# A neural network's forward pass on one core: query and value products of the head loop from split operands

## The chip, the core and the metric

One Trainium2 chip, one core (core 0). The metric is the device time of one execution in microseconds (us). Three runs of the kernel before gave a median of 2646.47 us, from 2644.33 to 2648.1.

## What is computed

Four blocks work on an input of 4 x 128 x 32 x 32: a convolution block, a dynamic convolution, an attention with a gated feed-forward block, and the block that matters here: an attention with 16 heads on 4 x 1024 tokens of 128 channels, and a mixture of experts behind it. The reference of that attention, cut to what the change touches:

```python
cq = _rms(x @ Wcq, q_norm_w)                    # query latents, 48 a token
qn = (cq @ Wq_nope).reshape(B, T, N_HEAD, NOPE) # 32 a head, Wq_rope gives 32 more, then turned
qr = _rope((cq @ Wq_rope)...)
q = jnp.concatenate([qn, qr], -1)
ckv = _rms(x @ Wckv, kv_norm_w)                 # key/value latents, 32 a token
v1 = (ckv @ Wv).reshape(B, T, N_HEAD, VDIM)     # 32 a head
o1 = _attn(q, k1, v1, causal)                   # all earlier keys
o2 = _attn(q, ks, vs)                           # 256 selected keys
o3 = _attn(q, kw, vw, winmask)                  # a window of 64 keys
o = g[:, 0] * o1 + g[:, 1] * o2 + g[:, 2] * o3
return o @ Wproj
```

## The kernel before

The program runs in stages with a barrier behind each: `stage_conv`, `stage_attn2`, `stage_ffn2`, `stage_latents` (L1652), `stage_heads` (L2185), `stage_ffn3`. Two of them are touched.

**`stage_latents`** makes, for each of the 4 batches, the layer norm, the query and key/value latents, the gates and the selection of 256 keys, and stores all in one DRAM tensor `latents`. DVE scales the latents into `CK` (L1866 to L1874), TensorE transposes `CK` to 112 rows (L1761), ScalarE copies them to `CF` [112, 1024] (L1820); rows 0 to 31 are the key/value latents, rows 32 to 63 the mean part of the values, rows 64 to 111 the query latents, all fp32. `CKS` holds the key/value latents split in two: a high part rounded to TensorE's fast fp32 type (called fp32r in the rows) and a low part, the remainder. SP stores five tiles a batch (L1699 XC, L1702 CF, L1705 gates, L1708 CKS, L1711 XS) and waits for all of them at the end; POOL does nothing after three memsets.

**`stage_heads`** makes 16 passes: 4 batches, and in each 4 groups of four heads. The first pass and what overlaps it run ahead of a hardware loop (`nc.Fori`), whose 15 turns each end one pass and begin the next; all engines follow one order of steps written out by hand, the string `ORDER` (L1971). A step with a plus sign belongs to the next pass: the query groups stand in it as `+a.q0` (ahead of `+near` work, behind `score.17.2`), `+a.q1` (behind `score.18.3`), `+a.q2` (behind `score.24.0`) and `+a.q3` (behind `score.3.0`), the value products of the causal branch as `v.v1.0` (at `score.4.1`) and `v.v1.1` (at `score.5.3`). A query group (`group`, L2388) is two fp32 products of 256 columns, CF's 112 rows by `WQ` [112, 256], whose rows 0 to 63 are zero; the same helper makes the window's and the selected keys' groups (`WKW`, `WKS`). A value product (`value_product`, L2416) is four fp32 products of 128 columns, CF by `WV` [112, 128], with zeros outside its 32 rows. An fp32 product shows as two MATMUL records, one of fp32r operands as one.

Scores are made from split operands (L2480 and L2481: `QH`, `QL` and the keys `K`, `K1B`), ScalarE takes their exponentials (`PT`, L2621), TensorE multiplies them with the values (L2500), and POOL adds the exponentials of the causal branch over the key tiles (`KT`, L2339), which TensorE turns into denominators (L2510, with `ones`). DVE rounds, normalises and gathers (`YB`, L2722), POOL adds the branches (`YA`, `YT`, L2345, L2348). SP loads the next pass's tiles behind step `load.next` (L2275: XS, WKS, XC, WKW, WQ, WVW, WVS) and behind `load.own` (L2284: CF, CKS, gates, WK1, WV), both long ahead of their use except in the first pass. At the stage's start TensorE runs 62 products of masks (`keep_clock`, L2524) while the first loads land, and DVE clears `WQ` and `WV` (L2753, L2755).

## Time and profile before

| | |
|---|---|
| median of 3 runs | 2646.47 us (2644.33 to 2648.1) |
| the profiled execution, its own time | 2643.02 us |
| its span; mean granted TensorE clock | 2641.1 us; 0.943 of full speed |
| PE, PEld busy | 2367.4 us (90%), 1718.4 us (65%) |
| DVE, ACT, POOL busy | 1814.2 (69%), 1413.0 (53%), 1285.8 us (49%) |
| DMA | 128.14 MB; HBM read 61.26, written 20.79 MB |
| latents' stage; head stage | from 505 to 638 us; from 638 to 2470 us |

The profile is one execution. PE is TensorE's matmuls, PEld its weight loads, DVE VectorE, ACT ScalarE, POOL GpSimd, SP SyncE, which here issues the transfers. Busy shares are means over stages with different limits, so a change is judged by the stage in which it lies and by the waits there: a row of the timeline ends with the idle time before it and what ended that.

### The profile page before, as it was taken

What the parts mean: (1) busy time and instruction counts of PE and PEld (TensorE: products, weight loads), DVE (VectorE), ACT (ScalarE), POOL (GpSimd) and SP (SyncE); (2) the same over time, 40 slices, a digit from 0 to 9 for tenths busy, and PEclk for the clock granted to TensorE, in tenths of its full rate; (3) what the DMA queues carried; (4) which work ended last, traced back from release to release, by engine and by line L of the source; (5) the groups of instructions that cost most, each with busy time, mean ns of one, the idle gap of its engine ahead of it and who ended that gap; (6) DMA issues with size and microseconds to landing.
All of it is one profiled execution on the core that took longest, in us unless ns stands there. A gap on an engine that the chain in (4) does not pass through costs nothing. (4 is left out here: it accounts for less than half of the span.)

```text
span 2641.1 us, 51557 instructions
## 1 busy us (share of the span) xinstructions
PE 2367.4 (90%) x16821; PEld 1718.4 (65%) x16821; DVE 1814.2 (69%) x3640; ACT 1413.0 (53%) x2489; POOL 1285.8 (49%) x972
## 2 busy tenths in 40 slices
PE   6889968666899999999999999999999999999767
PEld 4666645454667767677676676767667676675656
DVE  5868745585577686776867768676776867766436
ACT  2135544232565656656566565665657666575223
POOL 1016760000264746647365573755737557375445
PEclk8989988768999999999999999999999999999678
DMA  3040300013412111220212202122021220210233
GB/s 118 1 102 20 78 10 1 16 50 87 129 43 54 28 41 36 49 54 16 54 36 45 58 16 54 36 45 58 16 54 36 45 58 16 54 20 17 70 118 102
DMA packets 82189, 128.14 MB, mean 49 GB/s; under 512 B 15824, under 2 KB 58240, under 8 KB 81728
## 3 DMA queue, kind: packets, MB, share of 16 engines
q1 hardware_dynamic: 77616, 119.47, 17.9%
q0 software_dynamic: 3024, 7.43, 0.9%
q8 instruction: 46, 0.75, 0.1%
q10 hardware_dynamic: 1472, 0.24, 0.1%
q14 instruction: 31, 0.25, 0.0%
HBM read 61.26 MB, written 20.79 MB: 31 GB/s over the span
## 5 line engine op out<-in xcount | busy, mean ns | idle before, releaser
L2621 ACT ACTIVATE a_PT<-PS 128x512 f32<-128x512 f32 (+1 forms) x1104 | 584.4, 565 | 365.1 <-PE PS L2486 241.4
L2339 POOL TENSOR_TENSOR a_KT<-a_PT 128x256 f32<-128x256 f32 (+2 forms) x176 | 354.3, 2025 | 459.7 <-ACT a_PT L2621 451.2
L2339 POOL TENSOR_TENSOR a_KT<-a_KT,a_PT 128x2048 f32<-128x2048 f32 (+3 forms) x128 | 391.8, 3061 | 10.3 <-ACT a_PT L2621 1.0
L2690 DVE TENSOR_REDUCE a_NM<-PS 128x2 fp32r<-128x512 f32 (+2 forms) x512 | 290.8, 612 | 134.2 <-PE PS L2430 73.5
L2480 PE MATMUL PS<-a_QH,a_K 128*128 128x512 f32 (+3 forms) x768 | 293.1, 392 | 2.9 <-ACT a_PT L2621 2.8
L2702 DVE TENSOR_REDUCE a_MX<-PS 128x1 f32<-128x512 f32 (+3 forms) x432 | 265.6, 664 | 32.7 <-PE PS L2445 18.1
L2480 PE MATMUL PS<-a_QH,a_KSW 128*128 128x192 f32 (+3 forms) x832 | 264.5, 339 | 12.1 <-DVE a_NM L2690 10.5
L2445 PE MATMUL PS<-a_K,a_QH 128*128 128x512 f32 (+3 forms) x768 | 252.3, 404 | 9.4 <-DVE a_K L2677 8.1
L2481 PE MATMUL PS<-a_QL,a_K1B 76*128 76x512 f32 (+3 forms) x768 | 260.1, 349 | 0.0
L2430 PE MATMUL PS<-a_KSW,a_QH 128*128 128x256 f32 (+2 forms) x1024 | 198.8, 306 | 4.1 <-DVE a_QL L2674 4.1
L2430 PEld LDWEIGHTS PS<-a_KSW,a_QH 128*128 128x128 f32 x1024 | 164.0, 193 | 49.6 <-DVE a_NM L2690 19.5
L2327 POOL TENSOR_TENSOR a_TM<-a_R 128x128 f32<-128x128 f32 x288 | 124.1, 458 | 130.0 <-DVE a_R L2656 130.0
L2480 PEld LDWEIGHTS PS<-a_QH,a_KSW 128*128 128x128 f32 x832 | 160.4, 193 | 41.3 <-issue 13.5
L2677 DVE TENSOR_TENSOR a_KSW<-PS,a_KSW 64x512 fp32r<-64x512 f32 x160 | 110.3, 689 | 108.3 <-ACT a_KSW L2580 105.3
L2580 ACT ACTIVATE a_QH<-PS 64x512 fp32r<-64x512 f32 x256 | 151.5, 592 | 51.3 <-PE PS L2398 46.6
L2486 PE MATMUL PS<-masks,identb 128*128 128x128 bf16 (+3 forms) x592 | 172.2, 291 | 0.0
L2480 PEld LDWEIGHTS PS<-a_QH,a_K 128*128 128x128 f32 x768 | 149.0, 194 | 33.6 <-issue 14.5
L2445 PEld LDWEIGHTS PS<-a_K,a_QH 128*128 128x128 f32 x768 | 135.6, 193 | 45.5 <-DVE a_MX L2702 17.3
L2607 ACT ACTIVATE a_QL<-PS 12x1024 fp32r<-12x1024 f32 x128 | 130.1, 1017 | 60.7 <-PE PS L2460 58.3
L2481 PEld LDWEIGHTS PS<-a_QL,a_K1B 76*128 76x128 f32 x768 | 147.1, 192 | 9.6
L2656 DVE TENSOR_TENSOR a_R<-PS,a_angles 128x512 f32<-128x512 f32 x144 | 96.2, 687 | 72.9 <-ACT a_TM L2572 71.9
L2481 PE MATMUL PS<-a_QL,a_KWB 76*128 76x192 f32 (+2 forms) x576 | 141.1, 275 | 0.0
(434 smaller groups left out, 5223.2 us busy)
## 6 DMA issues: line engine op xcount, KB each, us to landing
a_KWB<-a_KSW SPq DMA_DIRECT2D x64, 256.0 KB, 3.3
a_K1B<-a_K SPq DMA_DIRECT2D x32, 512.0 KB, 4.9
a_XC<-latents SPq DMA_DIRECT2D x16, 512.0 KB, 3.8
a_CKS<-latents SPq DMA_DIRECT2D x16, 512.0 KB, 4.6
a_CF<-latents SPq DMA_DIRECT2D x16, 448.0 KB, 4.2
slots<-in_empty_slots SPq DMA_DIRECT2D x1, 5160.0 KB, 18.7
f_XB<-slots SPq DMA_DIRECT2D x8, 645.0 KB, 6.0
c_EX<-in_experts SPq DMA_DIRECT2D x1, 4608.0 KB, 18.0
```

What stands on the lines that cost most here:

```text
L2327: last = nc.gpsimd.tensor_tensor(TM[:, x, :, 32 + c:48 + c], r[:, :, 0, c:c + 16], r[:, :, 1, other:other + 16], ALU.add)
L2339: nc.gpsimd.tensor_tensor(total, one_in, other_in, ALU.add).then_inc(s["added"], 1)
L2430: last = nc.tensor.matmul(bank[:, m * w:(m + 1) * w], QH[:, h, i * 128:(i + 1) * 128], keys[x][:, h, c0:c0 + w], start=m == 0, stop=x == 1 ...
L2445: last = nc.tensor.matmul(bank[:, m * w:(m + 1) * w], QH[:, h0 + m, i * 128:(i + 1) * 128], K1[:, h0 + m, c0:c0 + w], start=m == 0, stop=n ...
L2480: nc.tensor.matmul(out, keys[x][:, h, c:c + 128], QH[:, h, start:start + w], start=m == 0, stop=False)
L2481: last = nc.tensor.matmul(out, upper[x][0:DH + ROWS, h, c:c + 128], QL[0:DH + ROWS, h, start:start + w], start=False, stop=mask is None an ...
L2486: last = nc.tensor.matmul(by_heads[:, :, 0:cols], identb[:, :], add[:, None, :].broadcast_to([128, each, cols]), start=False, stop=True)
L2580: last = nc.scalar.activation(odd_even({"q": QH, "w": KW, "s": KS}[g[0]], e, rows, tokens(g)), ring(key)[e * DH:(e + 1) * DH, :].rearrange ...
L2607: nc.scalar.activation(QL[DH:DH + ROWS, :, p * PAIR:(p + 1) * PAIR], turning(key)[DH:DH + ROWS, None, 0:PAIR].broadcast_to([ROWS, QUAD, PA ...
L2621: nc.scalar.activation(PT[:, to:to + width], turning(key)[:, 0:width], ACT.Exp).then_inc(s["taken"], 1)
L2690: nc.vector.tensor_reduce(NM[:, i, DH:].rearrange("p (h x) -> p h x", x=3)[:, h:h + 2, x], ring(key)[:, 0:2 * w].rearrange("p (h n) -> p h ...
L2702: nc.vector.tensor_reduce(out, ring(key)[:, 0:heads * w].rearrange("p (h n) -> p h n", h=heads), AX.X, ALU.max, negate=True).then_inc(s["r ...
```

## The change

**Operands.** `stage_latents` now makes `CQ` [128, 1024], the query latents twice: the mean multiply on DVE writes them twice into `CQ2` (768 elements in place of 384), TensorE transposes 128 rows, ScalarE copies all of them rounded into `CQ` and the lower 64 rows unrounded into `CF`, and POOL subtracts, so that rows 0 to 47 hold the high part and rows 64 to 111 the low part. The weights `wq3` and `wv` are loaded whole, twice (partitions 0 and 64), rounded by four activations of ScalarE ahead of the batch loop, their low parts made by two subtractions of POOL, and both parts kept in a new DRAM tensor `parted` [128, 3072], 1.5 MB, stored by two transfers at the end of the stage.

**Products.** A query product is two fp32r matmuls that add up in one bank, CQ by the high and CQ by the low part of the weights; a value product is CKS by the two parts of `WV`. `WQ` is now [128, 2, 256] (256 KB a load, before 48), `WV` [128, 2, 128] (128 KB, before 16), CQ 512 KB (CF was 448). The two memsets of DVE go. Nothing moves in `ORDER`.

```diff
-        CF, XS, row = sb("CF", [CKW + QR_, N]), sb("XS", [C, KEEP3]), rk["row"]
+        CF, CQ, XS, row = sb("CF", [128, N]), sb("CQ", [128, N], F32R), sb("XS", [C, KEEP3]), rk["row"]
...
+        CK2, CQ2 = sb("CK2", [128, NT, 2, CKW]), sb("CQ2", [128, NT, 2, CKW])
+        WQF, WVF = sb("WQF", [128, NQ, QUAD * DH]), sb("WVF", [128, NQ, QUAD * VD])
+        WQP, WVP = sb("WQP", [128, 2, NQ, QUAD * DH], F32R), sb("WVP", [128, 2, NQ, QUAD * VD], F32R)
...
+                wq, wv = d["wq3"][0:NQ * QR_, :], d["wv"][0:NQ * KR_, :]
+                for at in (0, CKW):
+                    sp.dma_start(WQF[at:at + QR_, :, :], wq.rearrange("(g p) c -> p g c", p=QR_)).then_inc(s["ld_parted"], 16)
+                    sp.dma_start(WVF[at:at + KR_, :, :], wv.rearrange("(g p) c -> p g c", p=KR_)).then_inc(s["ld_parted"], 16)
...
-                    sp.wait_ge(s["lt_copied"], b * 2 + 2)
+                    sp.wait_ge(s["lt_split"], b + 1)
...
-                    sp.dma_start(entry[0:CKW + QR_, N:2 * N], CF[:, :]).then_inc(s["archived"], 16)
+                    sp.dma_start(entry[:, N:2 * N], CQ[:, :].bitcast(F32)).then_inc(s["archived"], 16)
...
+                sp.wait_ge(s["parted_low"], 2)
+                sp.dma_start(parted[:, 0:2 * NQ * QUAD * DH], WQP[:, :, :, :].rearrange("p a g c -> p (a g c)").bitcast(F32))\
+                    .then_inc(s["parted_kept"], 16)
+                sp.dma_start(parted[:, 2 * NQ * QUAD * DH:], WVP[:, :, :, :].rearrange("p a g c -> p (a g c)").bitcast(F32))\
+                    .then_inc(s["parted_kept"], 16)
                 sp.wait_ge(s["archived"], (B + 1) * ARCHIVE)
+                sp.wait_ge(s["parted_kept"], 32)
...
+                for tile in (WQP[:, :, :, :], WVP[:, :, :, :], CQ2[:, :, :, :]):
+                    nc.gpsimd.memset(tile.bitcast(F32), 0.0).then_inc(s["blank"], 1)
+                pool.wait_ge(s["parted_high"], 4)
+                nc.gpsimd.tensor_tensor(WQP[0:QR_, 1, :, :], WQF[0:QR_, :, :], WQP[0:QR_, 0, :, :].bitcast(F32), ALU.subtract)\
+                    .then_inc(s["parted_low"], 1)
+                nc.gpsimd.tensor_tensor(WVP[0:KR_, 1, :, :], WVF[0:KR_, :, :], WVP[0:KR_, 0, :, :].bitcast(F32), ALU.subtract)\
+                    .then_inc(s["parted_low"], 1)
+                for b in range(B):
+                    pool.wait_ge(s["lt_copied"], b * 2 + 2)
+                    nc.gpsimd.tensor_tensor(CQ[CKW:, :], CF[CKW:, :], CQ[CKW:, :].bitcast(F32), ALU.subtract).then_inc(s["lt_split"], 1)
...
-                            last = nc.tensor.transpose(P[4 + half][0:CKW + QR_, t * 128:(t + 1) * 128],
-                                                       CK[:, 4 * half + t, :], ident[:, :])
+                            last = nc.tensor.transpose(P[4 + half][:, t * 128:(t + 1) * 128],
+                                                       CQ2[:, 4 * half + t, :, :].rearrange("p r c -> p (r c)"), ident[:, :])
...
+                act.wait_ge(s["ld_parted"], 64)
+                act.wait_ge(s["blank"], 2)
+                for at in (0, CKW):
+                    nc.scalar.activation(WQP[at:at + QR_, 0, :, :], WQF[at:at + QR_, :, :], ACT.Copy).then_inc(s["parted_high"], 1)
+                    nc.scalar.activation(WVP[at:at + KR_, 0, :, :], WVF[at:at + KR_, :, :], ACT.Copy).then_inc(s["parted_high"], 1)
...
-                        nc.scalar.activation(CF[:, half * HALF:(half + 1) * HALF], P[4 + half][0:CKW + QR_, :], ACT.Copy)\
-                            .then_inc(s["lt_copied"], 1)
+                        cols = slice(half * HALF, (half + 1) * HALF)
+                        nc.scalar.activation(CQ[:, cols], P[4 + half], ACT.Copy)
+                        nc.scalar.activation(CF[CKW:, cols], P[4 + half][CKW:, :], ACT.Copy).then_inc(s["lt_copied"], 1)
...
-                    nc.vector.tensor_tensor(CK[:, :, KR_ + VD:], CK[:, :, KR_ + VD:],
-                                            nw[:, None, 0:QR_].broadcast_to([128, NT, QR_]), ALU.mult)
+                    dve.wait_ge(s["blank"], 3)
+                    twice = [128, NT, 2, QR_]
+                    nc.vector.tensor_tensor(CQ2[:, :, :, 0:QR_], CK[:, :, None, KR_ + VD:].broadcast_to(twice),
+                                            nw[:, None, None, 0:QR_].broadcast_to(twice), ALU.mult)
...
-                                         (WQ[CKW:, :], d["wq3"][bass.ds(g * QR_, QR_), :]),
+                                         (WQ[:, :, :].bitcast(F32), wq[:, :, bass.ds(g, 1), :].rearrange("p a g c -> p a (g c)")),
...
-                        for dst, src in ((CF[:, :], entry[0:CKW + QR_, N:2 * N]),
+                        sp.wait_ge(s["ready"], 5)
+                        for dst, src in ((CQ[:, :].bitcast(F32), entry[:, N:2 * N]),
...
-                                         (WV[0:KR_, :], d["wv"][bass.ds(g * KR_, KR_), :])):
+                                         (WV[:, :, :].bitcast(F32), wv[:, :, bass.ds(g, 1), :].rearrange("p a g c -> p a (g c)"))):
...
-                    src, w = {"q": (CF, WQ), "w": (XC, WKW), "s": (XS, WKS)}[g[0]]
+                    src, *ws = {"q": (CQ, WQ[:, 0, :], WQ[:, 1, :]), "w": (XC, WKW[:, :]), "s": (XS, WKS[:, :])}[g[0]]
                     for j in range(2):
                         c = (2 * int(g[1:] or 0) + j) * 128
-                        last = nc.tensor.matmul(ring(key)[:, j * 256:(j + 1) * 256], src[:, c:c + 128], w[:, :],
-                                                start=True, stop=True)
+                        for n, w in enumerate(ws):
+                            last = nc.tensor.matmul(ring(key)[:, j * 256:(j + 1) * 256], src[:, c:c + 128], w,
+                                                    start=n == 0, stop=n == len(ws) - 1)
...
-                    src, w, nt = {"v1": (CF, WV, 4), "vw": (XC, WVW, 4), "vs": (XS, WVS, 2)}[kind]
+                    nt, src, *ws = {"v1": (4, CKS, WV[:, 0, :], WV[:, 1, :]), "vw": (4, XC, WVW[:, :]), "vs": (2, XS, WVS[:, :])}[kind]
                     for t in range(nt):
                         c = (4 * x + t) * 128
-                        last = nc.tensor.matmul(ring(key)[:, t * 128:(t + 1) * 128], src[:, c:c + 128], w[:, :],
-                                                start=True, stop=True)
+                        for n, w in enumerate(ws):
+                            last = nc.tensor.matmul(ring(key)[:, t * 128:(t + 1) * 128], src[:, c:c + 128], w,
+                                                    start=n == 0, stop=n == len(ws) - 1)
...
-                nc.vector.memset(WQ[0:CKW, :], 0.0).then_inc(s["ready"], 1)
                 nc.vector.memset(WKL[:, :, :].bitcast(F32), 0.0).then_inc(s["ready"], 1)
-                nc.vector.memset(WV[:, :], 0.0).then_inc(s["ready"], 1)
```

How TensorE's instructions stand at a query group of the loop (WQ the query weights, CF the latents, QH, QL, K, K1B the scores' operands). Before:

```order
L2480 MATMUL PS<-a_QH,a_K 128x512
L2481 MATMUL PS<-a_QL,a_K1B 128x512
L2242 REGISTER_ALU x2
L2388 MATMUL PS<-a_WQ,a_CF 128x256 x2
L2242 REGISTER_ALU
L2480 MATMUL PS<-a_QH,a_K 128x512
L2481 MATMUL PS<-a_QL,a_K1B 128x512
```

After:

```order
L2515 MATMUL PS<-a_QH,a_K 128x512
L2516 MATMUL PS<-a_QL,a_K1B 128x512
L2273 REGISTER_ALU x2
L2422 MATMUL PS<-a_WQ,a_CQ 128x256 x4
L2273 REGISTER_ALU
L2515 MATMUL PS<-a_QH,a_K 128x512
L2516 MATMUL PS<-a_QL,a_K1B 128x512
```

The two fp32 products have become four fp32r ones in the same place; the scores on both sides are where they were.

How SP's transfers stand between the last batch of the latents' stage and the first of the heads'. Before:

```order
L1708 DMA latents<-l_CKS 128x1024 [waits l3_ld,l3_ckt_split]
L1711 DMA latents<-l_XS 128x256 [waits l3_ld,l3_xs_copied]
L1686 UNCONDITIONAL_BRANCH [waits l3_archived]
L2262 UNCONDITIONAL_BRANCH [waits barrier_Pool_Activation_PE_DVE_SP_release]
L2307 DMA a_angles<-in_angles 128x512
L2275 DMA a_XS<-latents 128x256
L2275 DMA a_WKS<-in_wks 128x256
L2275 DMA a_XC<-latents 128x1024
L2275 DMA a_WKW<-in_wkw 128x256
L2275 DMA a_WQ<-in_wq 48x256
```

After:

```order
L1718 DMA latents<-l_XS 128x256 [waits l3_ld,l3_xs_copied]
L1720 DMA parted<-l_WQP 128x2048 [waits l3_parted_low]
L1722 DMA parted<-l_WVP 128x1024
L1689 UNCONDITIONAL_BRANCH [waits l3_parted_kept,l3_archived]
L2293 UNCONDITIONAL_BRANCH [waits barrier_Pool_Activation_PE_DVE_SP_release]
L2340 DMA a_angles<-in_angles 128x512
L2308 DMA a_XS<-latents 128x256
L2308 DMA a_WKS<-in_wks 128x256
L2308 DMA a_XC<-latents 128x1024
L2308 DMA a_WKW<-in_wkw 128x256
L2308 DMA a_WQ<-parted 128x2x256
```

Two stores and a wait for them stand ahead of the branch that ends the stage, and `WQ` comes from `parted`.

## Rows read from the trace of the kernel before

**Rows 1.** Windows, one pass: us, busy PE, PEld, DVE, ACT, POOL; PEclk, DMA, GB/s.

```profile
1134.20:1245.00 110.80, 107.12 (x792) 77.26 (x792) 80.66 (x136) 70.48 (x126) 65.27 (x52) 1.00 0.18 41
```

**Rows 2.** Timeline of PE at a query group: start, duration, shape, count.

```profile
1210.46 0.39 PE L2481 MATMUL PS<-a_QL,a_K1B 76*128 76x512 f32 x1
1210.69 1.03 PE L2388 MATMUL PS<-a_WQ,a_CF 112*128 112x256 f32 x4
...
1211.79 0.40 PE L2481 MATMUL PS<-a_QL,a_K1B 76*128 76x512 f32 x1
```

**Rows 3.** Timeline of PE, 256-column matmuls of split operands, same pass.

```profile
1235.85 0.28 PE L2480 MATMUL PS<-a_QH,a_K 128*128 128x256 f32 x1
1235.97 0.28 PE L2481 MATMUL PS<-a_QL,a_K1B 76*128 76x256 f32 x1
```

**Rows 4.** Timeline of PE, a value product.

```profile
1267.24 1.06 PE L2416 MATMUL PS<-a_WV,a_CF 112*128 112x128 f32 x8
```

**Rows 5.** Timeline of PE, 128-column matmuls of split operands.

```profile
733.89 0.27 PE L2481 MATMUL PS<-a_QL,a_KWB 76*128 76x128 f32 x1
734.00 0.28 PE L2480 MATMUL PS<-a_QH,a_KSW 128*128 128x128 f32 x1
```

**Rows 6.** Timeline of PE, later in that pass; idle before and releaser bracketed.

```profile
1241.16 1.03 PE L2388 MATMUL PS<-a_WQ,a_CF 112*128 112x256 f32 x4
...
1245.02 1.07 PE L2510 MATMUL PS<-a_KT,a_ones 128*32 128x512 f32 x8 [0.67 <-POOL a_KT L2339]
...
1252.05 1.13 PE L2388 MATMUL PS<-a_WQ,a_CF 112*128 112x256 f32 x4
...
1255.30 1.07 PE L2510 MATMUL PS<-a_KT,a_ones 128*32 128x512 f32 x8
```

**Rows 7.** Timeline of POOL, the same pass.

```profile
1216.28 4.56 POOL L2339 TENSOR_TENSOR a_KT<-a_PT 128x2048 f32<-128x2048 f32 x1 [2.11 <-ACT a_PT L2621]
...
1223.71 21.25 POOL L2339 TENSOR_TENSOR a_KT<-a_KT,a_PT 128x2048 f32<-128x2048 f32 x6
...
1249.13 1.27 POOL L2348 TENSOR_TENSOR a_YT<-a_YA,a_YB 128x512 f32<-128x512 f32 x1 [2.51 <-DVE a_YB L2722]
...
1252.41 2.76 POOL L2339 TENSOR_TENSOR a_KT<-a_PT,a_zero 128x512 f32<-128x512 f32 x4
```

**Rows 8.** Timeline of ACT, the same pass, first and last of five rows.

```profile
1210.55 1.58 ACT L2621 ACTIVATE a_PT<-PS 128x512 f32<-128x512 f32 x3 [0.28 <-POOL a_KT L2339]
...
1215.03 1.09 ACT L2621 ACTIVATE a_PT<-PS 128x512 f32<-128x512 f32 x2
```

**Rows 9.** Timeline of DVE in the latents' stage, 384 and 256 elements.

```profile
562.86 0.55 DVE L1872 TENSOR_TENSOR l_CK<-l_CK,l_nw 128x384 f32<-128x384 f32 x1
563.33 0.42 DVE L1874 TENSOR_TENSOR l_CK<-l_CK,l_nw 128x256 f32<-128x256 f32 x1
```

**Rows 10.** Timeline of ACT, latents' stage, ahead of batch 0's layer norm.

```profile
530.47 0.21 ACT L550 ACTIVATE l_ln_sd<-l_ln_va 128x8 f32<-128x8 f32 x1 [3.67 <-DVE l_ln_va L536]
```

**Rows 11.** Timelines of SP's queue and PE between the two stages.

```profile
635.46 0.33 SPq L1711 DMA_DIRECT2D latents<-l_XS  x1
...
638.14 10.23 PE L2524 MATMUL PS<-masks,identb 128*128 128x384 bf16 x62 [3.13 <-PEq L40]
```

**Rows 12.** DMA issues: count, KB each, median us to landing.

```profile
latents<-l_XC SPq DMA_DIRECT2D x4, 512.0 KB, 2.6
out_tokens<-T SPq DMA_DIRECT2D x1, 2048.0 KB, 7.5
latents<-l_XS SPq DMA_DIRECT2D x4, 128.0 KB, 1.7
```

**Rows 13.** Windows of the latents' stage, columns as in rows 1.

```profile
555.00:558.30 3.30, 0.99 (x6) 0.77 (x5) 2.30 (x14) 1.88 (x3) 0.00 (x0) 1.00 0.11 40
558.50:568.60 10.10, 6.85 (x31) 6.23 (x32) 9.64 (x27) 5.33 (x9) 0.00 (x0) 0.50 0.26 92
629.10:633.40 4.30, 4.26 (x10) 3.45 (x11) 1.30 (x2) 0.00 (x0) 0.00 (x0) 0.50 0.29 122
```

More of the change, by code:

```diff
@@ L1649, with stage_latents @@
 LATENT = 3 * N + KEEP3 + 8
-def stage_latents(nc, keep, P, T, ident, lohi, below, tri, latents, d):
+def stage_latents(nc, keep, P, T, ident, lohi, below, tri, latents, parted, d):
     with ExitStack() as ctx:
@@ L1681, in stage_latents @@
             "gsub", "gexp", "gate", "rms", "rms_std", "latent", "lt_ready", "lt_copied", "onehot", "xs_ready", "xs_copied",
+            "lt_split", "ld_parted", "blank", "parted_high", "parted_low", "parted_kept",
             "ck_twice", "ckt_ready", "ckt_round", "ckt_split", "pos", "archived")
@@ L2182, in before, with stage_heads @@
                     next((name for name in passed[:passed.index(key):-1] if same(name)), None))
-def stage_heads(nc, keep, PS, P, T, ident, identb, masks, turned, latents, d, slots, emptied):
+def stage_heads(nc, keep, PS, P, T, ident, identb, masks, turned, latents, parted, d, slots, emptied):
     with ExitStack() as ctx:
@@ L2205, in stage_heads @@
         YA, YT = sb("YA", [128, 2, HALF]), sb("YT", [128, HALF])
-        XC, CF, XS = sb("XC", [C, N]), sb("CF", [CKW + QR_, N]), sb("XS", [C, KEEP3])
+        XC, CQ, XS = sb("XC", [C, N]), sb("CQ", [128, N], F32R), sb("XS", [C, KEEP3])
         CKS = sb("CKS", [128, N], F32R)
-        WQ = sb("WQ", [CKW + QR_, QUAD * DH])
+        WQ = sb("WQ", [128, 2, QUAD * DH], F32R)
         WKW, WKS = sb("WKW", [C, QUAD * DH]), sb("WKS", [C, QUAD * DH])
@@ L2211, in stage_heads @@
         WKH, WKL = sb("WKH", [128, QUAD, DH], F32R), sb("WKL", [128, QUAD, DH], F32R)
-        WV, WVW, WVS = sb("WV", [CKW + QR_, QUAD * VD]), sb("WVW", [C, QUAD * VD]), sb("WVS", [C, QUAD * VD])
+        WV, WVW, WVS = sb("WV", [128, 2, QUAD * VD], F32R), sb("WVW", [C, QUAD * VD]), sb("WVS", [C, QUAD * VD])
         WP = sb("WP", [128, NQ, C])
@@ L2265, in load @@
                     entry = latents[bass.ds(b, 1), :, :].rearrange("b p n -> (b p) n")
+                    wq = parted[:, 0:2 * NQ * QUAD * DH].rearrange("p (a g c) -> p a g c", a=2, g=NQ)
+                    wv = parted[:, 2 * NQ * QUAD * DH:].rearrange("p (a g c) -> p a g c", a=2, g=NQ)
                     if name == "next":
@@ L2558, in _ @@
                 keep_clock(60)
-                pe.wait_ge(s["ready"], 7)
+                pe.wait_ge(s["ready"], 5)
                 one_pass(None, None)
@@ L2760, in _ @@
                 dve.wait_ge(s["ld"], 16)
-                dve.wait_ge(s["ready"], 7)
+                dve.wait_ge(s["ready"], 5)
                 one_pass(None, None)
@@ L2782, in program @@
         latents = nc.dram_tensor("latents", [B, 128, LATENT], F32, kind="Internal").ap()
+        parted = nc.dram_tensor("parted", [128, 2 * NQ * QUAD * (DH + VD)], F32, kind="Internal").ap()
         for stage, tiles in ((stage_conv, (P, T, ident, lohi, below, tri, identb, both, d)),
@@ L2785, in program @@
                              (stage_ffn2, (PS, P, T, ident, below, d)),
-                             (stage_latents, (P, T, ident, lohi, below, tri, latents, d)),
-                             (stage_heads, (PS, P, T, ident, identb, masks, turned, latents, d, slots, emptied)),
+                             (stage_latents, (P, T, ident, lohi, below, tri, latents, parted, d)),
+                             (stage_heads, (PS, P, T, ident, identb, masks, turned, latents, parted, d, slots, emptied)),
                              (stage_ffn3, (PS, P, T, ident, tri, d, slots, out))):
```

4 lines of the change are left out of this document (1 added, 3 removed).

## The prediction

> **What bounds the kernel now.** I read the busy time of one pass of the head loop first, then the chain of waits inside it, then both ends of the latents' stage, which the change lengthens. In a pass of 110.8 us TensorE is busy 107.1, ScalarE 70.5, POOL 65.3 [rows 1]. That looks like a kernel bound by TensorE, and sixteen passes are two thirds of the span. The reader should see in the next groups that it is a tie: POOL and ScalarE each hold stretches in which TensorE's lead is worth nothing.
>
> **The query products.** A query group is two fp32 products of 256 columns, each run as two records. From the start of the matmul ahead of the group to the start of the second one behind it 1211.79 - 1210.46 = 1.33 us pass [rows 2]; two of these steps are split-operand matmuls of 512 columns, 0.235 each (0.23 between the first two starts, which are rounded to 0.01), so the four records take 0.86 us, 0.215 each. The change issues four records too, but of rounded operands, and such a matmul of 256 columns is followed after 1235.97 - 1235.85 = 0.12 us [rows 3]. A group takes 0.48 instead of 0.86: 0.38 us less, times four groups and 16 passes (64) is **24.3 us of TensorE time**.
>
> **The value products** gain nothing. Eight fp32 records of 128 columns take 1.06 us [rows 4], less the last one's 0.275, over seven steps: 0.112 each, two per product. The rounded 128-column matmuls are 0.11 to 0.12 apart [rows 5], and the change issues two of those per product. At 256 records and 0 to 5 ns each that is 0 to +1.3 us; half of them (the second value product) come before work that waits for nothing else. I take +0.3. The Trainium skill (TensorE: Matmul & The Clock Gate, Back-to-back issue gap) gives about 81 ns for a 128-column matmul with its weight load in a stream; by that the values would save 256 x 0.031 = 8 us of TensorE, and the sum would be lower by up to as much. The trace disagrees at 0.11 us, and the sum goes by the trace.
>
> **What of the 24.3 us is on the path.** The four groups (q0 to q3) stand in one pass in this order, q0 at 1210.69, q2 at 1241.16 and q3 at 1252.05 [rows 2, 6].
> - q1 and q2 (up to 1241.16): POOL starts the exponentials' sums at 1216.28 after a wait for ScalarE and has no idle row again until 1244.97 (six additions of 21.25 us from 1223.71) [rows 7]. TensorE reaches the last denominators of the pass, waits 0.67 us for exactly that POOL result and starts at 1245.02 [rows 6]. Being 0.76 us earlier only turns 0.67 of waiting into 1.43. Worth 0.
> - q0 (1210.69): what lets POOL start at 1216.28 is an exponential of ScalarE. ScalarE was itself released by POOL at 1210.55, and its five rows from there to 1215.03 + 1.09 show no idle at all [rows 8]. The query group starts after that release, so it can't move ScalarE. Worth 0.
> - q3 (1252.05): DVE's chain behind the denominators lets POOL go at 1249.13, and POOL adds without a gap until 1252.41 + 2.76 = 1255.17; TensorE's next denominators start at 1255.30 [rows 6, 7]. Only 1255.30 - 1255.17, less a release of some 0.05, can come back: 0.08 a pass. Bounds 0 and 15 x 0.08 = 1.2 us; I take 0.
> - The first pass has no other pass beside it and its steps wait for one another; up to four times 0.38 = 1.5 us, at least 0. I take -1.0.
> So of 24.3 us I count **1.0**. After the groups, TensorE waits longer for POOL: what is late next is POOL's row of additions.
>
> **The latents' stage.** The mean multiply of the query latents writes them twice, 768 instead of 384 elements. DVE needs 0.55 us for 384 and 0.42 for 256 [rows 9], 1.0 ns an element: +0.40 us, in a DVE row without gaps that ends in the selection the next batch waits for. Four batches: **+1.6** (ends 1.2 and 2.0). ScalarE's extra copies in a batch (two of 64x512) stand in its own idle time before the row copies. Its four roundings of weights (1024, 512, 1024 and 512 elements) come once, before batch 0's layer norm: three activations of 512 took 1.58 us [rows 8], so 3072 elements take 3.2 us, where ScalarE has 3.67 us of idle [rows 10]. Cost 0; if that cover falls short, up to 0.5. POOL is idle in the stage; the query latents' store waits for its subtraction, some 3 us later than before, and two other stores of the batch still come after it. Cost 0.
>
> **The store at the end.** New and in the open: after the last batch SP issues 1.5 MB of parted weights, and the stage ends only when they have landed. Now the last store (128 KB) is issued at 635.46 and lands 1.7 us later [rows 12], and the next stage's first matmul starts at 638.14 [rows 11], 1.0 us after the landing. 512 KB land 2.6 us after their issue and 2048 KB after 7.5 [rows 12]; in between, 1536 KB need 5.9 us, from an issue at 635.8 (one issue behind), so 641.7; with the same 1.0 us behind it, 642.7: **+4.5**. The ends are +4.0 (slope of the larger store alone) and +6.4 (512 KB's rate throughout: 7.8 us).
>
> **The clock behind it.** TensorE now idles 3.1 us between the stages and its 62 warming matmuls run at full clock, 10.23 us [rows 11]. It will idle 7.6. Earlier in the stage, in a stretch in which TensorE was busy for 0.99 of 3.3 us, the granted clock was still 1.00, and in the next 10 us it was 0.50 (the lower of its two levels, 1.2 of 2.4 GHz) [rows 13]: I expect it at the lower level when the next stage begins. A dense stretch at the lower level later in this stage lasted 4.3 us, busy for 4.26 [rows 13], before the clock rose; at half speed the warming loses half of such a stretch: **+2.2** (ends 0, if the level is kept, and 3.4). The weights' and latents' loads of the heads grow by 384 KB, 208 KB of it ahead of the first group. They are hidden now, since the warming ends later than the loads land, and more so if it gets longer; 0, at worst +1.0. In the loop these loads are issued tens of us before use: 0.
>
> **Sum**: -1.0 + 0.3 + 1.6 + 4.5 + 2.2 = +7.6 us on the profiled execution's 2643.0, which lies 3.5 us below the median of 2646.5 of the runs. On the median: **2654.1 us**.
>
> **Rivals.** (A) *TensorE is the bound after all.* Its 97% in a pass speaks for it; then every group's 0.38 us counts and the cost is 8.6: 2646.5 - 24.3 + 8.6 = 2630.8, faster. The price of the whole change decides from 8.6 us, or 23 of 64 groups on the path. Against it: no group stands in a stretch that TensorE's lead would shorten [rows 6 to 8]. Chance 0.13. The Trainium skill (Perfetto Trace Analysis, Identifying the Most-Contended Engine) says to optimize the engine with the highest occupancy first, and that for TensorE matmul busy time misleads. Read by occupancy it stands for this rival; here rows 6 to 8 speak against it. (B) *The ends cost less*: the clock stays up (0 instead of 2.2), q3 gives back its 1.2 and the first pass its 1.5: -2.7 + 0.3 + 1.6 + 4.5 = +3.7, 2650.2, no change to tell. For it: the store's length is the only sure price. Chance 0.25. (C) *The ends cost more*: store 6.4, clock 3.4, loads late by 1.0, weights' roundings 0.5, DVE 2.0, values 1.3, nothing back: +14.6, 2661.1. Chance 0.04. Forecast: 0.58.
>
> **How the numbers follow.** A measurement of this kernel can tell about 0.2%, 5.3 us. Forecast and C are slower: 0.62 less the forecast's lower edge, 0.58. B and that edge, less a part of B in which some groups count as well: 0.27. A with that part: 0.15. The range reaches down into B with some gain in the loop (2643) and up to 2660, where the bounds of store and clock nearly add up; A and C's end stay out.
>
> **What would show it.** Right: the query rows at 0.12 us a record, TensorE's busy time some 20 us less, the wait for POOL at the last denominators of a pass up from 0.67 to about 1.4 us, a pass still 110.7; the next stage some 6 us later, its warming near 12.5 us. Wrong: passes of 109.2 us or so (A), or the store landing within 4 us of its issue.

## The result and the profile after

The kernel after takes **2671.6 us** (median of 4 runs, 2667.6 to 2677.4) against 2645.7 of the kernel before in the same runs: ratio 1.0103, 95% interval 1.009 to 1.0117. It is slower, as forecast, but by 26 us and not by 8, outside the range. The profiled executions differ by about as much: spans of 2669.3 and 2641.1 us, 28.2 apart.

From the page of the kernel after:

```profile
span 2669.3 us, 51584 instructions
...
PE 2366.1 (89%) x16821; PEld 1708.1 (64%) x16821; DVE 1818.2 (68%) x3638; ACT 1420.5 (53%) x2501; POOL 1301.8 (49%) x981
```

TensorE is busy for as long as before (2367.4), though its query groups became shorter. What ate that shows in the head loop. A turn of it, in the timeline of PE of the kernel after (start us, duration, shape, count, in brackets the idle time before and what ended it); L2422 is the query group, L2545 the denominators, L2451 the value product, L2559 nine products of masks (`keep_clock(9, bank)` in `near_scores`) that were there before and that the prediction passed over:

```profile
1234.34 0.82 PE L2422 MATMUL PS<-a_WQ,a_CQ 128*128 128x256 f32 x4
...
1260.15 1.06 PE L2545 MATMUL PS<-a_KT,a_ones 128*32 128x512 f32 x8 [1.27 <-POOL a_KT L2372]
...
1270.42 1.06 PE L2545 MATMUL PS<-a_KT,a_ones 128*32 128x512 f32 x8 [0.28 <-POOL a_KT L2372]
...
1273.29 1.01 PE L2451 MATMUL PS<-a_WV,a_CKS 128*128 128x128 f32 x8
1276.00 2.91 PE L2559 MATMUL PS<-masks,identb 128*128 128x384 bf16 x9 [1.71 <-DVE a_QL L2709]
...
1293.17 1.06 PE L2545 MATMUL PS<-a_KT,a_ones 128*32 128x512 f32 x8
```

The same place in the kernel before, and the windows over the nine products (columns as in rows 1), first of before, then of after:

```profile
1258.16 1.06 PE L2416 MATMUL PS<-a_WV,a_CF 112*128 112x128 f32 x8
1260.87 1.64 PE L2524 MATMUL PS<-masks,identb 128*128 128x384 bf16 x9 [1.66 <-DVE a_QL L2674]
```

```profile
1261.00:1262.20 1.20, 1.20 (x9) 0.70 (x8) 0.35 (x1) 1.16 (x3) 0.00 (x0) 1.00 0.00 1
```

```profile
1276.60:1278.60 2.00, 2.00 (x9) 0.99 (x7) 1.38 (x2) 1.98 (x4) 0.00 (x0) 0.50 0.00 0
```

Read them in this order. The query group is shorter as forecast (0.82 for 1.03 us in the first row), and its time lies where forecast: the wait for POOL ahead of the denominators grew from 0.67 us [rows 6] to 1.27, and 0.28 us appeared ahead of the next ones. Then comes the new thing. Behind a wait of 1.7 us, which both kernels have, **the granted clock is at the lower of its two levels (1.2 of 2.4 GHz)** in the kernel after; the nine products take 2.91 us and not 1.64, and from the denominators of the first half to the next ones it is 22.7 us and not 21.1. Of the 15 turns, 12 show this in the kernel after and 2 in the kernel before. Ten more at 1.6 us are 16 us. The place in time has a part in which turns: in six turns one behind the other the nine products take 3.06, 2.91, 2.64, 2.38, 2.08 and 1.64 us. Three of them, in the timeline of PE of the kernel after:

```profile
1163.71 3.06 PE L2559 MATMUL PS<-masks,identb 128*128 128x384 bf16 x9 [1.69 <-DVE a_QL L2709]
...
1500.73 2.38 PE L2559 MATMUL PS<-masks,identb 128*128 128x384 bf16 x9 [1.71 <-DVE a_QL L2709]
...
1725.37 1.64 PE L2559 MATMUL PS<-masks,identb 128*128 128x384 bf16 x9 [1.71 <-DVE a_QL L2709]
```

So 12 of 15 is a count of these turns and not a chance that each of them has by itself.

The rest comes from the latents' stage. DVE and POOL there, ahead of batch 0's layer norm, in the timelines of the kernel after:

```profile
531.11 2.32 DVE L529 TENSOR_TENSOR l_ln_tmp<-l_ln_st 128x8 f32<-128x8 f32 x1
533.46 1.18 DVE L531 TENSOR_SCALAR l_ln_mv<-l_ln_tmp 128x8 f32<-128x8 f32 x1
```

```profile
531.07 2.33 POOL L1735 TENSOR_TENSOR l_WQP<-l_WQF,l_WQP 48x1024 fp32r<-48x1024 f32 x1 [20.89 <-ACT l_WVP L1835]
533.36 1.25 POOL L1737 TENSOR_TENSOR l_WVP<-l_WVF,l_WVP 32x512 fp32r<-32x512 f32 x1
```

Two operations of DVE on 8 elements, 0.17 us each in the kernel before, last as long as POOL's two subtractions beside them: 3.2 us in DVE's row. And the end of the stage, in SP's queue and PE:

```profile
640.23 0.33 SPq L1718 DMA_DIRECT2D latents<-l_XS  x1
640.61 0.42 SPq L1720 DMA_DIRECT2D parted<-l_WQP  x1
641.08 0.44 SPq L1722 DMA_DIRECT2D parted<-l_WVP  x1
646.89 0.34 SPq L2340 DMA_DIRECT2D a_angles<-in_angles  x1
```

```profile
646.92 12.50 PE L2559 MATMUL PS<-masks,identb 128*128 128x384 bf16 x62 [7.14 <-PEq L40]
```

From the last latents' store to the next stage are 6.7 us and not 2.7 [rows 11], and the 62 warming products take 12.50 and not 10.23 us.

The 28.2 us of the two profiled executions, by the starts of the same instructions in both:

| place | us |
|---|---|
| up to batch 0 of the latents: earlier stages in this execution, loads | +1.5 |
| DVE beside POOL's subtractions | +3.2 |
| rest of the latents' stage, the doubled multiply among it | +0.1 |
| store at its end | +4.0 |
| warming at the lower clock | +2.3 |
| first pass: its query groups; the clock once | -0.9; +1.8 |
| 10 more turns at the lower clock | +16.1 |

The +1.8 is a difference: the kernel before has a stretch at the lower clock in its first pass too, but ahead of the stall. Its value product takes 1.91 us there (at 703.42), and the wait behind it is 0.07 us and not 1.66.

### The profile page after: what moved, and what is told of

Read it like the earlier page. It is cut to its first block and busy times, and to the rows that moved or that the text cites. A ratio compares the mean times of both kernels' runs of the same rounds, so it can differ in the third digit from the quotient of the medians.

```text
span 2669.3 us, 51584 instructions
## 1 busy us (share of the span) xinstructions
PE 2366.1 (89%) x16821; PEld 1708.1 (64%) x16821; DVE 1818.2 (68%) x3638; ACT 1420.5 (53%) x2501; POOL 1301.8 (49%) x981
## 5 line engine op out<-in xcount | busy, mean ns | idle before, releaser
L2515 PE MATMUL PS<-a_QH,a_KSW 128*128 128x192 f32 (+3 forms) x832 | 265.9, 341 | 12.1 <-DVE a_NM L2725 10.5
L2465 PE MATMUL PS<-a_KSW,a_QH 128*128 128x256 f32 (+2 forms) x1024 | 205.5, 311 | 4.6 <-DVE a_QL L2709 4.6
L2712 DVE TENSOR_TENSOR a_KSW<-PS,a_KSW 64x512 fp32r<-64x512 f32 x160 | 110.3, 690 | 106.6 <-ACT a_KSW L2615 103.5
L2749 DVE STREAM_TRANSPOSE a_RT<-PS 128x512 f32<-128x512 f32 x96 | 68.8, 717 | 111.0 <-PE PS L2545 111.0
```

The source lines that it names most:

```text
L2465: last = nc.tensor.matmul(bank[:, m * w:(m + 1) * w], QH[:, h, i * 128:(i + 1) * 128], keys[x][:, h, c0:c0 + w], start=m == 0, stop=x == 1 ...
L2515: nc.tensor.matmul(out, keys[x][:, h, c:c + 128], QH[:, h, start:start + w], start=m == 0, stop=False)
```

## The experiments

Three theories were set against each other for the clock: IDLE (TensorE idles more ahead of the stall), OPERANDS (the rounded products themselves), PLACE (only where the turns fall in time). The number of turns with the lower clock is counted in each trace by the 22.7 us in place of 21.1.

### Which part lets the clock fall (e1 to e3)

e1, query products in fp32 again:

```diff
-src, *ws = {"q": (CQ, WQ[:, 0, :], WQ[:, 1, :]),
+src, *ws = {"q": (CQ.bitcast(F32), WQ[:, 0, :].bitcast(F32)),
```

> The kernel after, but each query product is again one fp32 product (CQ by the high part of the query weights; their low part is left out), so a group takes 0.86 us again and not 0.48. In the kernel after the granted clock falls to its lower level behind the 1.7 us stall of TensorE in 12 of the loop's 15 turns, in the kernel before in 2, at 1.6 us each. Theory IDLE (the shorter groups make TensorE wait about 1 us more in the 20 us ahead of that stall, 3.3 instead of 2.3 us): low in at most 4 of 15 turns, waits ahead of the denominators back to 0.67 and 0, 2671.6 - 16 = about 2655 us. Theory OPERANDS, by the value products (the rounded value products just ahead of the stall count for less than fp32 ones): low in 12 of 15, about 2672 us. Theory PLACE (the turns begin 11 us later than before and fall otherwise against the chip's own rhythm): low in about 12 of 15 too.

e2, value products in fp32 again:

```diff
-nt, src, *ws = {"v1": (4, CKS, WV[:, 0, :], WV[:, 1, :]),
+nt, src, *ws = {"v1": (4, CKS.bitcast(F32), WV[:, 0, :].bitcast(F32)),
```

> The kernel after, but each causal value product is again one fp32 product (CKS by the high part of the value weights; their low part is left out); the query groups stay rounded and short. IDLE: nothing changes, low in about 12 of 15 turns, about 2671 us. OPERANDS by the value products: low in at most 4 of 15, about 2655 us. PLACE: about 12 of 15.

e3, query products issued twice:

```diff
+if g[0] == "q":
+    for w in ws:
+        nc.tensor.matmul(ring(key)[:, j * 256:(j + 1) * 256], src[:, c:c + 128], w, start=True, stop=True)
```

> The kernel after with every query product issued twice, all of it rounded operands: eight matmuls of 0.12 us a group, 0.96 us, a little more than the 0.86 of the kernel before. IDLE: the waits go back to about 0.6 and 0 us, low in at most 4 of 15 turns, about 2655 us although TensorE has 31 us more to do. OPERANDS, by the query products (rounded ones count for less): low in 12 of 15 still, about 2672. If TensorE were the bound of the turn, each turn would grow by up to 1.9 us, 31 us in all: 2700.

| kernel | median us | ratio to before (95%) | turns with the lower clock |
|---|---|---|---|
| e1 query products fp32 | 2672.8 | 1.0091 (1.006 to 1.0122) | 12 of 15 |
| e2 value products fp32 | 2651.3 | 1.002 (1.0003 to 1.0038) | 0 of 15 |
| e3 query products twice | 2682.1 | 1.0102 (1.0049 to 1.0155) | 15 of 15 |

The value product and the nine products behind it, in the timelines of PE of e1, e2 and e3, with the denominators ahead of it in e1 and e2:

```profile
1265.39 1.07 PE L2545 MATMUL PS<-a_KT,a_ones 128*32 128x512 f32 x8 [0.68 <-POOL a_KT L2372]
...
1278.52 1.01 PE L2451 MATMUL PS<-a_WV,a_CKS 128*128 128x128 f32 x8
1281.23 2.34 PE L2559 MATMUL PS<-masks,identb 128*128 128x384 bf16 x9 [1.71 <-DVE a_QL L2709]
```

```profile
1264.30 1.06 PE L2545 MATMUL PS<-a_KT,a_ones 128*32 128x512 f32 x8 [0.29 <-POOL a_KT L2372]
...
1267.16 1.06 PE L2451 MATMUL PS<-a_WV,a_CKS 128*128 128x128 f32 x8
1269.88 1.64 PE L2559 MATMUL PS<-masks,identb 128*128 128x384 bf16 x9 [1.66 <-DVE a_QL L2709]
```

```profile
1285.74 3.05 PE L2562 MATMUL PS<-masks,identb 128*128 128x384 bf16 x9 [1.67 <-DVE a_QL L2712]
```

IDLE falls. e1 has the waits of the kernel before (0.68, and none ahead of the second denominators) and the lower clock in 12 turns; e2 has the waits of the kernel after and never the lower clock. A wait of 1.66 and not 1.7 us isn't it either: e3's second pass has 1.66 us, like e2's, and nine products of 3.06 us behind it. PLACE alone falls by the kernels taken together: with rounded value products and the nine products behind the stall the clock is low in 12, 12, 15 and 11 turns (the kernel after, e1, e3 and e6 below), with fp32 ones in 2 and 0 (the kernel before, e2), though their first passes lie up to 17 us apart. e2 and the kernel after can be compared at one place, their first passes, whose value products start at 713.13 and 713.03 us: upper clock in e2, lower in the kernel after. Later their turns drift apart, to 20 us. It is the value products, as OPERANDS said, though they last as long as before; which of the turns are hit depends on their place in time as well, and how is left open. e3 shows besides that TensorE isn't the bound: with 29 us more of work for it (60 groups of 0.48) its 15 turns took 6.6 us more than those of the kernel after, and 3 more turns at the lower clock are 5 of these. The 10.5 us between the medians say less, with single times of e3 from 2660.6 to 2687.1.

### Kind of operand or columns (e5)

e5, value products of 256 columns a matmul:

```diff
+o, wide = (min(t, 2) * 128, 256) if kind == "v1" else (t * 128, 128)
+w = WV[:, :, :].rearrange("p a c -> p (a c)") if kind == "v1" else w
-last = nc.tensor.matmul(ring(key)[:, t * 128:(t + 1) * 128], src[:, c:c + 128], w,
+last = nc.tensor.matmul(ring(key)[:, o:o + wide], src[:, c:c + 128], w,
```

> The kernel after, but the eight rounded matmuls of a causal value product stream 256 columns each (both parts of the weights at once) and not 128; their results overlap in the bank and the values are left wrong, the time is what is asked. The rows of the kernel before have 256 columns of rounded operands following each other after 0.12 us and 128 after 0.11, so a product takes about 0.08 us longer for twice the columns. Theory KIND (it is the kind of operand: rounded value products ahead of the stall let the clock fall, fp32 ones do not): low in 12 to 15 of 15 turns, about 2672 us. Theory COLUMNS (a rounded 128-column matmul holds TensorE's row for 0.11 us, but streams no longer than half of what an fp32 one does, and it is this that was taken away ahead of the stall): low in at most 2 of 15, about 2652 us.

Measured: 2651.5 us, ratio 1.0024 (1.001 to 1.0037), lower clock in **0 of 15** turns. The two rows in its timeline of PE:

```profile
1269.29 1.12 PE L2453 MATMUL PS<-a_WV,a_CKS 128*128 128x256 f32 x8
1272.01 1.64 PE L2561 MATMUL PS<-masks,identb 128*128 128x384 bf16 x9 [1.60 <-DVE a_QL L2711]
```

KIND falls, and COLUMNS is what is left of the theories: with rounded operands of twice the columns, in 1.12 us for 1.01, the clock stays up. A row of busy time therefore says less than it seems to: eight rounded matmuls of 128 columns fill 1.01 us, but so do, nearly, eight of 256. The fp32 records of 128 columns are as far apart as the rounded ones (0.11 us), while of 256 columns they are 0.215 against 0.12 apart [rows 2, 3]; the columns alone thus don't set the distance of the rounded ones of 128. That rounded matmuls of 128 columns are busy for less of that distance is a conclusion from these distances; no row shows it. e5's product is also 0.1 us longer and its wait as much shorter, 1.60 us; e5 by itself doesn't exclude that this alone decides, but e2, whose product is 0.05 us longer with a wait of 1.66, speaks against it.

### Repairs (e4, e6, e7, e8)

e4, the nine products moved ahead of the value product, into the stall:

```diff
-                    if i == 4 and n == 0:
-                        keep_clock(9, bank)
...
+                    if kind == "v1" and x == 0:
+                        keep_clock(9, ring(key))
```

> The kernel after with the nine mask products that keep the clock up moved from behind the 1.7 us stall to ahead of the first value product, in that product's bank, so that they run in the stall (1.47 us of its 1.7). IDLE: the clock stays at its upper level in all turns, -12 x 1.6 = -20 us: about 2652; and where the nine products stood on the path, up to 1.47 us more a turn, down to 2629. OPERANDS: the clock still falls in most turns, 2665 or more. A rival on the price: ScalarE, busy without a gap there, or DVE takes up the 1.47 us, and only the 20 us come back.

Measured: 2644.6 us, ratio 1.0004 (0.9984 to 1.0024), lower clock in no turn, which takes 110.3 us (110.7 before). Rows of its timeline of PE:

```profile
1263.54 1.64 PE L2559 MATMUL PS<-masks,identb 128*128 128x384 bf16 x9
1264.88 1.14 PE L2453 MATMUL PS<-a_WV,a_CKS 128*128 128x128 f32 x8
1266.34 0.47 PE L2465 MATMUL PS<-a_KSW,a_QH 128*128 128x256 f32 x2 [0.32 <-DVE a_QL L2709]
...
1267.87 0.50 PE L2515 MATMUL PS<-a_QH,a_KSW 128*128 128x512 f32 x1 [0.59 <-ACT a_PT L2656]
```

The 20 us of the clock came back. The expectation had this for IDLE, and for OPERANDS a clock that falls still; that line missed: the value products are rounded here too, and the clock falls behind them only where the stall behind them is empty. The rival on the price was right: of the 1.47 us only 0.4 is won, the rest returns as waits for DVE and ScalarE.

e6, in the latents' stage; the bodies are moved whole:

```diff
                     nc.gpsimd.tensor_tensor(CQ[CKW:, :], CF[CKW:, :], ...).then_inc(s["lt_split"], 1)
+                    if b == 0:
+                        pool.wait_ge(s["parted_high"], 4)
...
                     sp.dma_start(entry[:, 3 * N:3 * N + KEEP3], XS[:, :]).then_inc(s["archived"], 16)
+                    if b == 1:
+                        sp.wait_ge(s["parted_low"], 2)
...
```

> The kernel after with two moves in the latents' stage: POOL's two subtractions of the weights behind its subtraction for batch 0, and the two stores of the parted weights behind the stores of batch 1. Theory PORT (in the kernel after DVE's additions of 8 elements at 531.11 and its scaling at 533.46 took 2.32 and 1.18 us and not 0.17, just as long as POOL's two subtractions ran, 2.33 and 1.25): DVE's row there is 0.17 again and the stage is 3.2 us shorter up to its last store. Rival QUEUE (it is ScalarE's four roundings, 3.2 us ahead of the square root at 531.01): nothing is won there. Both: the 4.0 us of the store at the end go, the next stage starts 3.1 us after TensorE's last matmul again and its 62 mask products take 10.2 and not 12.5 us. Together -3.2 - 4.0 - 2.3 = -9.5: about 2662 us with the clock still falling in 12 to 15 of 15 turns of the loop; 2665 by QUEUE.

e8 is e4 and e6 together, e7 is e4's move in the kernel before:

> The kernel before with the nine mask products moved ahead of the first value product, as in e4. There e4's turns went from 110.71 us (upper clock) to 110.3. Here the clock fell in 2 of 15 turns at 1.65 us; if the fill does the same: -3.3 - 15 x 0.43 = -9.7: about 2635 us. If the fills only helped because the rounded value products had taken something away: 2641 or more.

> The kernel after with both repairs, the nine mask products ahead of the first value product (e4) and the two moves in the latents' stage (e6). e4 took 2644.6; less 9.5 (PORT) is 2635 us, less 6.3 (QUEUE) is 2638. Against e7, the kernel before with the fill, it shows what the rounded products themselves are worth in the head loop: by the wait for POOL nothing, so both within 3 us of each other; if TensorE were the bound of the turn, 24 us less than e7.

Measured: e6 2665.1 us (ratio 1.0068, 1.0043 to 1.0092; lower clock in 11 of 15), e7 2640.7 (0.9975, 0.9957 to 0.9992), e8 2640.7 (0.9985, 0.9968 to 1.0001). e6 comes out at QUEUE's number, e7 5.7 us and e8 3 to 6 us above what was expected. The store and the warming came back whole: e8 goes from the last latents' store to the next stage in 2.7 us and warms in 10.23. The 3.2 us of DVE didn't, and the reason is the best evidence for PORT. DVE's two operations of 8 elements take 0.17 us again, though ScalarE's four roundings stand where they were, so QUEUE falls. But the subtractions now meet others, in the timelines of DVE and POOL of e8:

```profile
541.71 2.54 DVE L1097 SCALAR_TENSOR_TENSOR l_rk_same<-l_rk_row,l_rk_col,below 128x128 bf16<-128x128 f32 x1
...
544.19 1.33 DVE L1097 SCALAR_TENSOR_TENSOR l_rk_same<-l_rk_row,l_rk_col,below 128x128 bf16<-128x128 f32 x1
```

```profile
541.75 2.35 POOL L1740 TENSOR_TENSOR l_WQP<-l_WQF,l_WQP 48x1024 fp32r<-48x1024 f32 x1
544.07 1.31 POOL L1742 TENSOR_TENSOR l_WVP<-l_WVF,l_WVP 32x512 fp32r<-32x512 f32 x1
```

Their six sisters take 0.34 us. DVE's scans (L1094) of 640 to 128 columns, beside which POOL's other subtraction ran (2.35 us from 539.33), weren't slowed: 0.88 us for 640 columns, as in the kernel before. The Trainium skill (SBUF — State Buffer, Who interferes with whom) says that a DVE instruction with two inputs in SBUF contends with a GpSimd instruction that reads SBUF, and that one with at most one such input doesn't, outside the fast two-port modes. The rows of the two kinds above agree. By it the cure is to put the subtractions beside the scans, which have one input in SBUF.

e7's and e8's turns are alike, 110.3 us: the rounded products are worth nothing measurable in them, with all clocks up. That the medians agree to 0.01 us is chance, since each scatters by more than 10 us.

### Where the query groups' time went (e9, e10)

Both leave out half of POOL's additions; e9 is otherwise e7, and e10 is e8.

```diff
+total, one_in, other_in = (x[:, :, 0:w // 2] for x in (total, one_in, other_in))
 nc.gpsimd.tensor_tensor(total, one_in, other_in, ALU.add).then_inc(s["added"], 1)
```

> e7 (the kernel before with the fill ahead) with each of POOL's additions of exponentials in the head loop run over the first half of its columns; the other half of the denominators is left at 1 and wrong, the time is what is asked. Theory POOL (TensorE's two waits ahead of the denominators are for POOL's additions): both waits go and a turn of 110.3 us becomes shorter, by 0.7 us or more. Rival ELSE (ScalarE's or DVE's chain ends the turn as late without POOL): the turn stays 110.3.

> e8 (the kernel after with both repairs) with the same halved additions. POOL: here TensorE waited 1.33 + 0.28 us a turn for POOL and its query groups are 1.5 us a turn shorter; with POOL out of the way the turn is shorter than e9's by up to 1.5 us, 24 us over 16 turns. ELSE: no difference between e10 and e9, as between e8 and e7.

Measured: e9 **2612.2 us** (0.9872, 0.9845 to 0.99), e10 **2592.4 us** (0.9808, 0.9787 to 0.9829). One turn of each, as windows, e9 first:

```profile
915.62:1024.94 109.32, 107.19 (x800) 77.11 (x796) 80.70 (x136) 70.65 (x127) 41.45 (x51) 1.00 0.18 42
```

```profile
909.75:1017.90 108.15, 105.95 (x800) 75.98 (x796) 80.57 (x136) 70.33 (x127) 41.41 (x51) 1.00 0.19 46
```

POOL stands. With half of POOL's additions out of the way no wait is left ahead of the denominators, and only then do the rounded products pay: 1.2 us a turn, 20 us between the medians, of the 24.3 that the prediction counted as TensorE's time.

### Having it without leaving work out (e11 to e16)

e11 and e12 move denominators in `ORDER`, and they keep four of the nine products of masks ahead of the value product; here is the move of the first half's:

```diff
-+add.6 +sum.0 +rope.q3 +norm.0
++add.6 +rope.q3
-score.4.1 v.v1.0 near.4.0
+score.4.1 v.v1.0 sum.0 near.4.0 norm.0
```

> e8 with three moves. In the latents' stage POOL's two subtractions of the weights start as soon as DVE has the latents, so that they run beside DVE's scans with one tile in SBUF and not beside its operations with two; e6 and e8 had moved the collision there (128-column operations of DVE at 541.71 and 544.19 of e8 took 2.54 and 1.33 us, not 0.35). In the head loop the denominators of the first half (sum.0) go from the end of a turn into TensorE's stall behind the first value product of the next, their normalisation on DVE behind the first window scores, and the mask products there from nine to four. By PORT all DVE rows of 128 columns are 0.35 us again and the latents' stage is 3.2 us shorter than e8's. In the loop, theory COVER (the 0.28 us wait for POOL and the 1.06 us of denominators leave the path, and ScalarE's and DVE's chain of the last query groups starts that much earlier): a turn of 109.0 us for 110.3, 20 us in all; with PORT 2640.7 - 23 = about 2618 us. Rival SHIFT (POOL's next additions or DVE's normalisation, which comes later, take it back): the turn stays at 110.3, about 2637 us.

> e11, and the denominators of the last half (sum.5), ahead of which TensorE waits 1.3 us for POOL, go behind the next scores (one step, about 0.5 us of TensorE's work). COVER: 0.5 us of that wait is filled, a turn 0.4 us shorter than e11's, about 6 us in all. SHIFT: the normalisation and POOL's additions behind it come no later, since the denominators start when POOL is done in both; if nothing else on TensorE's path gets earlier, the turn is as long as e11's.

Measured: e11 2672.2 us (1.01, 1.0076 to 1.0124), e12 2658.9 (1.0044, 1.0025 to 1.0063). In the latents' stage PORT held: DVE's rows are 0.34 us and the stage is 3.3 us shorter than e8's. In the loop SHIFT held, and worse. With DVE's normalisation late TensorE waits for the bank that it frees; e11's two turns at the upper clock take 111.7 us and not 110.3. In its 13 others the clock falls behind that wait (in e12 in 6). Whether the wait or the five products of masks that are gone let it fall, neither run tells apart. From e11's timeline of PE, and the window there:

```profile
1156.42 0.50 PE L2518 MATMUL PS<-a_QH,a_KSW 128*128 128x512 f32 x1 [0.66 <-ACT a_PT L2659]
...
1158.57 0.80 PE L2518 MATMUL PS<-a_QH,a_KSW 128*128 128x512 f32 x1 [0.94 <-DVE a_RT L2752]
```

```profile
1158.00:1160.00 2.00, 1.43 (x4) 1.24 (x5) 1.80 (x4) 0.43 (x2) 0.00 (x0) 0.59 0.00 0
```

e13 leaves the loop as in e8 and keeps the placed subtractions; e14 and e15 move only the last half's denominators, by one step and by two, and e16 does e14's move in e7:

```diff
-add.27 sum.5 norm.5
-+score.0.1
+add.27
++score.0.1 sum.5 norm.5
```

> e8 with POOL's two subtractions of the weights beside DVE's scans, as in e11, and the head loop as in e8: the kernel after with its three costs repaired (the store at the end, the collision on DVE, the clock). By e11's latents' stage 3.3 us less than e8, whose median was 2640.7: about 2637 us, turns of 110.3 us, clock low in none. If one of the three causes is not a cause of its own, it stays at 2640 or more.

> e13 with the denominators of the last half one step later, behind the next scores, and nothing else of e12. The query groups' time went into the 1.33 us wait for POOL ahead of them; e12's turns were 0.5 us shorter than e11's by this move. COVER: the wait falls to 0.6 us and the turn to 109.8, 7 us in all: about 2630 us. SHIFT: the turn stays at 110.3, 2637.

> e14 with the denominators two steps later. COVER: the whole wait of 1.3 us is filled, the turn is 109.2 us, 15 us in all: about 2622 us, unless the normalisation behind the denominators then holds up POOL's next additions (SHIFT), which would show as a longer wait ahead of the first half's denominators (0.28 us now).

> e7, the kernel before with the fill ahead, with the denominators of the last half one step later, as e14. It waits 0.69 us for POOL there. COVER: most of it is filled, 0.5 us a turn, 7 us in all: about 2634. The rounded products of e14 are then worth nothing still, e14 and this one within 5 us; they pay only where more of the wait is filled than the kernel before has (e15).

| kernel | median us | ratio to before (95%) | turn us |
|---|---|---|---|
| e13 | 2634.3 | 0.995 (0.9926 to 0.9975) | 110.3 |
| e14 | 2636.1 | 0.996 (0.9945 to 0.9975) | 110.4 |
| e15 | 2634.9 | 0.9961 (0.9945 to 0.9976) | 110.35 |
| e16 | 2634.7 | 0.9958 (0.9941 to 0.9976) | 110.35 |

e13 settles the costs: with the three repaired the kernel after is 9.6 us faster than the kernel before, and **beats both**. e14 to e16 settle the loop for SHIFT, since their turns stay at 110.35 to 110.4 us; that e16's median is the one that COVER gave, 2634, is luck. The two denominators of a turn, in the timelines of PE of e13 and of e15:

```profile
1131.52 1.06 PE L2548 MATMUL PS<-a_KT,a_ones 128*32 128x512 f32 x8 [1.31 <-POOL a_KT L2375]
...
1141.80 1.06 PE L2548 MATMUL PS<-a_KT,a_ones 128*32 128x512 f32 x8 [0.29 <-POOL a_KT L2375]
```

```profile
1129.88 1.06 PE L2548 MATMUL PS<-a_KT,a_ones 128*32 128x512 f32 x8
...
1140.16 1.06 PE L2548 MATMUL PS<-a_KT,a_ones 128*32 128x512 f32 x8 [1.48 <-POOL a_KT L2375]
```

The wait of 1.31 us is gone from its place and 1.2 of it stands ahead of the next denominators. Two waits for the same engine can't be filled one by one; POOL's row sets the turn. e16, without the rounded products, is as fast as e13, so what e13 wins it wins by the fill and not by the change. (e7 has turns of 110.3 us too; the 6 us between its median and e16's are most likely scatter of another stage, see the end: four of e7's times lie between 2632.8 and 2634.3.)

## Why the prediction was wrong

- **What bounds the loop: right.** POOL holds the turn. The wait at the last denominators was forecast to go from 0.67 to about 1.4 us and went to 1.27 to 1.38, and e9 and e10 show it from the other side. Rival A fell: e3 gave TensorE 29 us more to do in the turns and they took 6.6 us longer, 5 of them by the clock.
- **A group 0.48 instead of 0.86: right.** Four records are 0.12 us apart, as [rows 3] said. The sign of the worth of the groups, "1.0 of 24.3", was right as well (first pass -0.9, turns 0). Two other signs of being right stayed out: TensorE's busy time fell by 1.3 us and not by some 20, and most turns took 112.35 and not 110.7 us, both by the clock in the next point.
- **"The value products gain nothing": this step failed.** It costed them at +0.3 us by the distance of their rows, which didn't change (0.112 us before and after), and looked at no other effect; the clock in the loop, its waits being as long as before, stood in the sum at nothing. They are what lets the clock fall behind the stall, 12 turns of 15 in place of 2, 16 us, and once more in the first pass, 1.8 us. With them in fp32 again (e2) the kernel takes 2651.3 us, inside the range. The hint was in the trace: 2 turns of 15 of the kernel before have it too, and nine products of masks stand there only to keep the clock up. A count of the turns' lengths, and not the reading of one turn, would have shown a place on the edge.
- **The latents' stage, +1.6 by DVE's doubled multiply: mis-sized at both ends.** The multiply took 0.95 us for 0.55, but the waits behind it took it back: +0.1 in all. POOL's subtractions, costed at 0 as POOL "is idle in the stage", cost 3.2 us on DVE. The step looked at what POOL waits for and not at what runs on DVE beside it. ScalarE's roundings cost nothing, as said, though not in the idle time that was named: they stand ahead of its square root, whose result DVE needs only at 537.6.
- **The store +4.5: right, measured +4.0.** This is the lower end as given; worked from 7.5 us for 2048 KB, 1536 KB take 5.6 us, and the end would be +4.3. The two issues at 640.61 and 641.08 (4.8 us to landing) and 1.0 us behind it make up the 646.92 us at which the next stage begins. **The clock behind it +2.2: right, measured +2.3.**
- Sum: forecast +7.6; the terms that it named came to -0.9 + 0.1 + 4.0 + 2.3 = 5.5. Missing were 3.2 for DVE and 17.9 for the clock in the loop and its first pass. The 1.5 us left of the 28.2 lie ahead of the places that the change touches or in its loads, and no run tells these apart.

## What to carry to other kernels

When an edit gives TensorE narrower or fewer matmuls near a stall, price the clock too: look at every repetition of that place in the trace for the granted clock, not at one, since a place where it falls in 2 of 15 turns is an edge. A row's length doesn't tell what it does for the clock: eight rounded matmuls of 128 columns took 1.01 us, eight of 256 took 1.12. Filling products kept the clock up in all 15 turns when they ran in the stall (e4) and took 1.64 to 3.06 us when they stood behind it. A wait that an edit fills is worth something only if it doesn't come back at the next place that waits for the same engine. And before giving POOL new work, look at which DVE operations run beside it, those with two inputs in SBUF first.
